# A conditioned residual kernel: loads cut into 8 KB rows, and one ring of pairs split into two

## The chip, the cores and the metric

The kernel runs on one core of a Trainium2 chip. The metric is the device time of one execution in microseconds; three runs of the kernel before gave 642.07, 642.13 and 642.19 us, so the median is 642.13 us. Beside them one execution was taken with the hardware profiler: its own time was 642.29 us and its trace spans 640.4 us from the first instruction to the last.

## What is computed

128 samples of 128 channels by 2048 steps go through two residual channel maps. Each sample picks its own matrix out of 16 for the first and out of 32 for the second; the second adds a bias. Everything is float32.

```python
def _L0_cond_ref(x, weights, condition):
    W = weights[condition]
    return jnp.einsum('bct,bcd->bdt', x, W)

def _L1_cond_ref(x, subjects, weights, biases):
    w = weights[subjects]
    b = biases[subjects]
    out = jnp.einsum('bct,bcd->bdt', x, w)
    return out + jnp.transpose(b, (0, 2, 1))

x = x + _L0_cond_ref(x, L0_cond_weights, itok_B_0_15)            # x: (128, 128, 2048)
x = x + _L1_cond_ref(x, itok_B_0_31, L1_cond_weights, L1_cond_biases)
```

Both maps together are one product per sample with the matrix (I + W0)(I + W1), plus a bias. x is 134.2 MB and is read once; the result is as large and is written once.

## The kernel before

**Pairs and their layout.** The 128 samples are taken two at a time: 64 pairs q, each 2 MB in and 2 MB out. `x_pairs` (line 35) lays a pair over the 128 partitions so that partitions 0 to 63 hold the even sample and 64 to 127 the odd one, and each partition holds two neighbouring channels, which lie side by side in memory: a row of 16 KB. `out_pairs` (line 36) is the same for the stores. A pair lives in one of eight slots of the tile `xt`, 2 x 2048 float32 (16 KB) in each partition. The result of a pair is written into the slot its input came from.

**SyncE (SP, lines 103 to 110)** issues the loads: the two weight tensors, then x pair by pair. The first eight go out at once; each later one waits until the store of the pair eight before it has landed (`stored[slot]`, line 109), since it goes into the same slot.

**GpSimd (POOL, lines 112 to 138)** adds the identity to the two matrices that each sample picks, into `map0T` and `map1`, two pairs deep.

**TensorE (PE, lines 140 to 211)**: `combine` (line 150) multiplies the two matrices of both samples of the next pair into the last 512 columns of `acc1`; ScalarE copies the useful blocks into `both`. `term` (line 158) is one product over 64 channels, 512 steps wide: for each sample k, each half u of the channels and each chunk j of 512 steps, so 16 a pair, two of which (k=0 and k=1) use different halves of the array at the same time. The even sample collects in PSUM tile `acc0`, the odd one in `acc1`. `pair` (line 163) is the order of one pair: eight terms of the low 1024 columns, the combine for the next pair, eight terms of the high columns. A float32 matmul of the program stands as two MATMUL records in the trace, so a pair has 32 records of line 159 and 4 of line 154.

**VectorE (DVE, lines 222 to 233)** moves `acc0` out into `xt` with the bias, two instructions for each half of the columns. **ScalarE (ACT, lines 243 to 267)** does the same with `acc1` (line 251), copies the combined maps (lines 246 and 247), and issues the store of the pair (line 265) when both engines are done with it. At the end it waits for all stores.

The order of the work is written out by hand on every engine; between engines it is set by semaphores. The DMA queue of SP, which carries all x loads, is q1 in the trace, and ACT's, which carries the stores, is q10. Both run on the same 16 DMA engines.

Of the kernel before, what the change touches and what calls it, by code (L numbers as in the profile page):

```python
# [5 lines left out]
def conditioned_residual_kernel(  # L6
# [18 lines left out]
    HC = C // 2  # L25
    CHUNK = 512
    HALF = T // 2
    SLOTS = 8
    PAIRS = B // 2
    TURNS = PAIRS // SLOTS  # L30
# [4 lines left out]
    x_pairs = x.rearrange("(q k) (i u) t -> q (k i) (u t)", k=2, u=2)  # L35
# [3 lines left out]
    with ctx:  # L39
# [20 lines left out]
        map0T = sb("map0T", [C, 2, 2, 2, HC])  # L60
# [22 lines left out]
        maps_ready = [sem(f"maps_ready{s}") for s in range(SLOTS)]  # L83
        combined = sem("combined")
        both_ready = [sem(f"both_ready{s}") for s in range(SLOTS)]
        lo_done0 = sem("lo_done0")
        lo_done1 = sem("lo_done1")
        hi_done0 = sem("hi_done0")
        hi_done1 = sem("hi_done1")

        lo_out = [sem(f"lo_out{s}") for s in range(SLOTS)]
        hi_out = [sem(f"hi_out{s}") for s in range(SLOTS)]
        x_loaded = [sem(f"x_loaded{q}") for q in range(SLOTS)]
        stored = [sem(f"stored{q}") for q in range(SLOTS)]

        w0T_v = w0T_sb[:, :, :].rearrange("p s (i u) -> p s u i", u=2)
# [5 lines left out]
        @block.sync  # L102
        def _(sp):
            sp.dma_start(w0T_sb[:, :, :], w0T).then_inc(w0_loaded, LOAD)
            sp.dma_start(w1_sb[:, :, :], w1).then_inc(w1_loaded, LOAD)
            for q in range(PAIRS):
                slot = q % SLOTS
                if q >= SLOTS:
                    sp.wait_ge(stored[slot], LOAD * (q // SLOTS))
                sp.dma_start(xt[:, slot, :], x_pairs[q, :, :]).then_inc(x_loaded[slot], LOAD)  # L110

        @block.gpsimd
        def _(pool):
# [9 lines left out]
            GROUP = 16  # L123
            for b in range(B):
                if b % GROUP == 0:
                    _, i0 = nc.values_load_multi_w_load_instructions(  # L126
                        cond_sb[0:1, 0, b:b + GROUP], engines=[POOL], min_val=0, max_val=S0 - 1,
                        skip_runtime_bounds_check_because="conditions index the maps")
                    _, i1 = nc.values_load_multi_w_load_instructions(  # L129
                        cond_sb[0:1, 1, b:b + GROUP], engines=[POOL], min_val=0, max_val=S1 - 1,  # L130
                        skip_runtime_bounds_check_because="conditions index the maps")
                q, k = b // 2, b % 2
                if q >= 2 and k == 0:

                    pool.wait_ge(combined, q - 1)
                nc.gpsimd.tensor_tensor(map0T[:, q % 2, :, k, :], w0T_v[:, bass.ds(i0[b % GROUP], 1), :, :], ident_v, ALU.add)  # L136
                nc.gpsimd.tensor_tensor(map1[:, q % 2, k, :, :], w1_v[:, bass.ds(i1[b % GROUP], 1), :, :], ident_v,  # L137
                                        ALU.add).then_inc(maps_ready[q % SLOTS], 1)

        @block.tensor  # L140
        def _(pe):
# [8 lines left out]
            def combine(slot, ready):  # L150

                pe.wait_ge(maps_ready[slot], ready)
                for u in range(2):
                    last = nc.tensor.matmul(acc1[:, CB + u * 2 * C:CB + (u + 1) * 2 * C],  # L154
                                            map0T[:, slot % 2, u, :, :], map1[:, slot % 2, :, :, :], start=True, stop=True)
                last.then_inc(combined, 1)

            def term(acc, k, u, buf, slot, j):
                return nc.tensor.matmul(acc[:, j * CHUNK:(j + 1) * CHUNK], both[k * HC:(k + 1) * HC, buf, u, :],  # L159
                                        xt[k * HC:(k + 1) * HC, slot, u * T + j * CHUNK:u * T + (j + 1) * CHUNK],  # L160
                                        start=u == 0, stop=u == 1)

            def pair(slot, outs, outs_before, next_maps, next_both, loads, begins, ends):

                buf = slot % 2
                prev, next = (slot - 1) % SLOTS, (slot + 1) % SLOTS
                if begins:
                    pe.wait_ge(both_ready[0], 1)

                pe.wait_ge(x_loaded[slot], loads)  # L170
                term(acc0, 0, 0, buf, slot, 0)
                term(acc1, 1, 0, buf, slot, 0)
                term(acc0, 0, 1, buf, slot, 0)
                term(acc1, 1, 1, buf, slot, 0)
                term(acc0, 0, 0, buf, slot, 1)
                term(acc1, 1, 0, buf, slot, 1)
                term(acc0, 0, 1, buf, slot, 1).then_inc(lo_done0, 1)
                term(acc1, 1, 1, buf, slot, 1).then_inc(lo_done1, 1)
                if not begins:
                    pe.wait_ge(hi_out[prev], outs_before)  # L180
                if not ends:
                    combine(next, next_maps)
                term(acc0, 0, 0, buf, slot, 2)
                term(acc1, 1, 0, buf, slot, 2)
                term(acc0, 0, 1, buf, slot, 2)
                term(acc1, 1, 1, buf, slot, 2)
                term(acc0, 0, 0, buf, slot, 3)
                if not ends:

                    pe.wait_ge(both_ready[next], next_both)  # L190
                term(acc1, 1, 0, buf, slot, 3)
                term(acc0, 0, 1, buf, slot, 3).then_inc(hi_done0, 1)
                if not ends:
                    pe.wait_ge(lo_out[slot], outs)
                term(acc1, 1, 1, buf, slot, 3).then_inc(hi_done1, 1)
# [99 lines left out]
```

## Time and profile before

| | |
|---|---|
| median of three runs | 642.13 us |
| profiled execution, its own time | 642.29 us |
| its span | 640.4 us |
| bytes moved by DMA | 271.82 MB, mean 424 GB/s |
| busy share: PE, DVE, ACT, POOL | 84%, 51%, 52%, 19% |
| mean granted TensorE clock | 0.986 of full speed |
| issue to landing, median: x load, store | 24.5 us, 42.9 us |

The page counts an engine as busy while one of its instructions runs. For the DMA engines it gives a share as well: the time of their packets over the time of 16 engines. A packet of this kernel is one row of one partition, and small packets beside them carry the semaphore updates. The clock is full as long as TensorE works; the mean is below one because it falls to half in the last 15 us, when TensorE has nothing left to do.

### The profile page before, as it was taken

What the parts mean: (1) busy time and instruction counts of PE and PEld (TensorE: products, weight loads), DVE (VectorE), ACT (ScalarE), POOL (GpSimd) and SP (SyncE); (2) the same over time, 40 slices, a digit from 0 to 9 for tenths busy, and PEclk for the clock granted to TensorE, in tenths of its full rate; (3) what the DMA queues carried; (4) which work ended last, traced back from release to release, by engine and by line L of the source; (5) the groups of instructions that cost most, each with busy time, mean ns of one, the idle gap of its engine ahead of it and who ended that gap; (6) DMA issues with size and microseconds to landing.
All of it is one profiled execution on the core that took longest, in us unless ns stands there. A gap on an engine that the chain in (4) does not pass through costs nothing.

```text
span 640.4 us, 6061 instructions
## 1 busy us (share of the span) xinstructions
PE 538.4 (84%) x2308; PEld 234.3 (37%) x2308; DVE 329.2 (51%) x259; ACT 333.5 (52%) x385; POOL 124.2 (19%) x263
## 2 busy tenths in 40 slices
PE   1899999999889889888898898888988988988860
PEld 0344444444334333333333333333333333433320
DVE  0266666666554455455545554555455445545550
ACT  0366666666555465455554654555555545545550
POOL 2322222222122122121221221211212212112000
PEclk9999999999999999999999999999999999999995
DMA  8999999999999999999999999999999999999996
GB/s 363 433 415 427 431 432 426 431 433 428 432 433 427 432 434 427 431 434 427 432 434 426 433 435 426 432 433 428 433 431 428 433 431 430 431 433 428 434 429 262
DMA packets 18931, 271.82 MB, mean 424 GB/s; under 512 B 2241, under 2 KB 2274, under 8 KB 2274
## 3 DMA queue, kind: packets, MB, share of 16 engines
q1 hardware_dynamic: 9504, 137.37, 50.3%
q10 hardware_dynamic: 9410, 134.26, 49.0%
q8 instruction: 7, 0.11, 0.1%
q14 instruction: 10, 0.08, 0.0%
HBM read 137.40 MB, written 134.22 MB: 424 GB/s over the span
## 4 chain that ended last, share of the span: by engine, by line
DMA 64%; PE 29%; DVE 3%; POOLq 0%; ACT 0%; issue 0%; DVEq 0%; POOL 0%; SPq 0%; ACTq 0%
DMA out_dram<-xt 40%; PE acc L159 25%; DMA xt<-in_x_dram 23%; PE acc L154 4%; DMA w_sb<-in_w_dram 1%; DVE xt L224 1%; DVE xt L226 1%; DVEq L39 0%; ACT L246 0%; POOLq L126 0%; POOLq L129 0%; POOL map0T L136 0%; POOL map L137 0%; ACT both L247 0%; ACT both L246 0%
## 5 line engine op out<-in xcount | busy, mean ns | idle before, releaser
L159 PE MATMUL acc<-xt,both 64*128 64x512 f32 x2048 | 472.5, 603 | 67.9 <-DMA xt<-in_x_dram 65.7
L251 ACT ACTIVATE xt<-acc,bias_of 64x1024 f32<-64x1024 f32 x256 | 283.7, 1108 | 270.1 <-PE acc L159 267.7
L159 PEld LDWEIGHTS acc<-xt,both 64*128 64x128 f32 x2048 | 189.8, 188 | 319.0 <-issue 211.5
L224 DVE TENSOR_SCALAR xt<-acc,bias_of 64x1024 f32<-64x1024 f32 x128 | 163.3, 1276 | 278.2 <-PE acc L159 278.2
L226 DVE TENSOR_SCALAR xt<-acc,bias_of 64x1024 f32<-64x1024 f32 x128 | 165.0, 1289 | 1.9
L136 POOL TENSOR_TENSOR map0T<-w0T_sb,ident 128x128 f32<-128x128 f32 x128 | 65.6, 513 | 465.8 <-PE acc L154 454.0
L154 PE MATMUL acc<-map,map0T 128*128 128x256 f32 x256 | 73.3, 409 | 1.2 <-POOL map L137 1.2
L137 POOL TENSOR_TENSOR map<-w_sb,ident 128x128 f32<-128x128 f32 x128 | 65.7, 513 | 0.0
L154 PEld LDWEIGHTS acc<-map,map0T 128*128 128x128 f32 x256 | 43.9, 191 | 53.0 <-issue 36.7
L247 ACT ACTIVATE both<-acc 64x256 f32<-64x256 f32 x64 | 24.3, 380 | 0.8
L246 ACT ACTIVATE both<-acc 64x256 f32<-64x256 f32 x64 | 24.2, 377 | 0.8
L246 ACT ACT_TABLE_LOAD x1 | 1.3, 1283 | 17.4 <-PE acc L154 17.4
L145 PE MATMUL acc<-ident,bias_sb 128*32 128x128 f32 x2 | 0.6, 418 | 10.8 <-DMA bias_sb<-in_bias_dram 10.8
L215 DVE TENSOR_TENSOR onehot<-cond_rep,row 32x128 f32<-32x128 int32 x1 | 0.3, 279 | 12.6 <-DMA cond_rep<-in_conds_dram 12.6
L145 PEld LDWEIGHTS acc<-ident,bias_sb 128*32 128x32 f32 x2 | 0.2, 142 | 10.8 <-DMA bias_sb<-in_bias_dram 10.8
L148 PE MATMUL acc<-onehot,biasT 32*128 32x128 f32 x2 | 0.8, 481 | 1.9 <-DVE biasT L217 1.9
L148 PEld LDWEIGHTS acc<-onehot,biasT 32*128 32x128 f32 x2 | 0.5, 304 | 2.3 <-DVE onehot L215 2.3
L219 DVE COPY bias_of<-acc 128x128 f32<-128x128 f32 x1 | 0.3, 292 | 0.9 <-PE acc L148 0.9
L217 DVE COPY biasT<-acc 32x128 f32<-32x128 f32 x1 | 0.3, 278 | 0.0
L117 POOL TENSOR_SCALAR_AFFINE_SELECT ident<-ident 128x128 f32<-128x128 f32 x1 | 0.3, 283 | 0.0
L114 POOL MEMSET ident<- 128x128 f32 x1 | 0.2, 204 | 0.3 <-POOLq L284 0.3
L115 POOL IOTA row<- 32x128 int32 x1 | 0.2, 224 | 0.0
(4 smaller groups left out, 0.4 us busy)
## 6 DMA issues: line engine op xcount, KB each, us to landing
xt<-in_x_dram SPq DMA_DIRECT2D x64, 2048.0 KB, 24.5
out_dram<-xt ACTq DMA_DIRECT2D x64, 2048.0 KB, 42.9
w_sb<-in_w_dram SPq DMA_DIRECT2D x1, 2048.0 KB, 9.4
w0T_sb<-in_w0T_dram SPq DMA_DIRECT2D x1, 1024.0 KB, 4.8
cond_sb<-in_conds_dram ACTq DMA_DIRECT2D x1, 1.0 KB
bias_sb<-in_bias_dram ACTq DMA_DIRECT2D x1, 16.0 KB, 9.4
cond_rep<-in_conds_dram ACTq DMA_DIRECT2D x1, 16.0 KB, 10.8
```

Of the source, the lines that this page charges most:

```text
L117: nc.gpsimd.affine_select(out=ident[:, :], in_=ident[:, :], compare_op=ALU.not_equal, fill=1.0, base=0, pattern=[[-1, C]], channel_multipl ...
L136: nc.gpsimd.tensor_tensor(map0T[:, q % 2, :, k, :], w0T_v[:, bass.ds(i0[b % GROUP], 1), :, :], ident_v, ALU.add)
L137: nc.gpsimd.tensor_tensor(map1[:, q % 2, k, :, :], w1_v[:, bass.ds(i1[b % GROUP], 1), :, :], ident_v, ALU.add).then_inc(maps_ready[q % SLO ...
L145: nc.tensor.matmul(acc0[0:S1, 0:C], bias_sb[:, :], ident[:, :], start=True, stop=True).then_inc(turned, 1)
L148: nc.tensor.matmul(acc1[:, 0:B], biasT[:, :, :], onehot[:, :], start=True, stop=True).then_inc(picked, 1)
L154: last = nc.tensor.matmul(acc1[:, CB + u * 2 * C:CB + (u + 1) * 2 * C], map0T[:, slot % 2, u, :, :], map1[:, slot % 2, :, :, :], start=Tru ...
L159: return nc.tensor.matmul(acc[:, j * CHUNK:(j + 1) * CHUNK], both[k * HC:(k + 1) * HC, buf, u, :], xt[k * HC:(k + 1) * HC, slot, u * T + j ...
L224: nc.vector.tensor_scalar(xt[0:HC, q % SLOTS, a:a + HALF], acc0[0:HC, a:a + HALF], bias_of[0:HC, 2 * q:2 * q + 1], None, ALU.add)
L226: return nc.vector.tensor_scalar(xt[0:HC, q % SLOTS, T + a:T + a + HALF], acc0[HC:C, a:a + HALF], bias_of[HC:C, 2 * q:2 * q + 1], None, AL ...
L246: nc.scalar.activation(both[0:HC, q % 2, :, :], crossed[0:HC, :, 0, :], ACT.Identity)
L247: nc.scalar.activation(both[HC:C, q % 2, :, :], crossed[HC:C, :, 1, :], ACT.Identity).then_inc(both_ready[q % SLOTS], 1)
L251: return nc.scalar.activation(xt[HC:C, q % SLOTS, v * T + a:v * T + a + HALF], acc1[v * HC:(v + 1) * HC, a:a + HALF], ACT.Identity, bias=b ...
```

## The change

The loads and the stores no longer share a buffer. x goes into a tile `xin` of six pairs, in which a partition is one channel and holds both samples of the pair, 2048 steps each: a row in memory is 8 KB, and a pair has 256 of them. Results go into a tile `xout` of four pairs, in the layout of before, with 128 rows of 16 KB. A product now runs over all 128 channels at once: four a sample, eight a pair, one after the other. The combine makes the two 128 x 128 blocks that are used and no others, and ScalarE copies them with one instruction.

SP issues load q when TensorE has finished pair q - 6 (`hi_done1`). TensorE waits before its second product of pair q for the store of pair q - 4. Semaphores for slots become semaphores for twelve places of a group; the loop body on TensorE covers twelve pairs in place of eight, and four pairs follow it.

```diff
-    SLOTS = 8
+    IN, OUT = 6, 4
+    GROUP = 12
...
-    x_pairs = x.rearrange("(q k) (i u) t -> q (k i) (u t)", k=2, u=2)
+    x_pairs = x.rearrange("(q k) c t -> c q k t", k=2)
     out_pairs = out.rearrange("(q k) (i u) t -> q (k i) (u t)", k=2, u=2)
...
-        xt = sb("xt", [C, SLOTS, 2 * T])
+        xin = sb("xin", [C, IN, 2, T])
+        xout = sb("xout", [C, OUT, 2 * T])
...
             for q in range(PAIRS):
-                slot = q % SLOTS
-                if q >= SLOTS:
-                    sp.wait_ge(stored[slot], LOAD * (q // SLOTS))
-                sp.dma_start(xt[:, slot, :], x_pairs[q, :, :]).then_inc(x_loaded[slot], LOAD)
+                if q >= IN:
+
+                    sp.wait_ge(hi_done1, q - IN + 1)
+                sp.dma_start(xin[:, q % IN, :, :], x_pairs[:, q, :, :]).then_inc(x_loaded[q % GROUP], LOAD)
...
-                nc.gpsimd.tensor_tensor(map0T[:, q % 2, :, k, :], w0T_v[:, bass.ds(i0[b % GROUP], 1), :, :], ident_v, ALU.add)
-                nc.gpsimd.tensor_tensor(map1[:, q % 2, k, :, :], w1_v[:, bass.ds(i1[b % GROUP], 1), :, :], ident_v,
-                                        ALU.add).then_inc(maps_ready[q % SLOTS], 1)
+                nc.gpsimd.tensor_tensor(map0T[:, q % 2, k, :], w0T_sb[:, bass.ds(i0[b % BATCH], 1), :], ident[:, :], ALU.add)
+                added = nc.gpsimd.tensor_tensor(map1[:, q % 2, k, :, :], w1_v[:, bass.ds(i1[b % BATCH], 1), :, :], ident_v, ALU.add)
+                if k == 1:
+                    added.then_inc(maps_ready[q % GROUP], 1)
...
+            def combine(k, p):
+                return nc.tensor.matmul(acc1[:, CB + k * C:CB + (k + 1) * C], map0T[:, p % 2, k, :], map1[:, p % 2, k, :, :],
+                                        start=True, stop=True)
+
+            def term(acc, k, p, j):
+                return nc.tensor.matmul(acc[:, j * CHUNK:(j + 1) * CHUNK], both[:, p % 2, k, :],
+                                        xin[:, p % IN, k, j * CHUNK:(j + 1) * CHUNK], start=True, stop=True)
+
+            def pair(p, turn, turn_before, turn_after, loads, stores, begins, ends):
+
+                prev, next = (p - 1) % GROUP, (p + 1) % GROUP
+                if begins and p == 0:
                     pe.wait_ge(both_ready[0], 1)
...
+                pe.wait_ge(x_loaded[p], loads)
+                term(acc0, 0, p, 0)
+                if not (begins and p < OUT):
+
+                    pe.wait_ge(stored[(p - OUT) % GROUP], stores)
+                term(acc0, 0, p, 1).then_inc(lo_done0, 1)
+                if not (begins and p == 0):
+                    pe.wait_ge(hi_out0[prev], turn_before)
+                term(acc0, 0, p, 2)
+                if not ends:
+                    pe.wait_ge(maps_ready[next], turn_after)
+                term(acc0, 0, p, 3).then_inc(hi_done0, 1)
+                if not (begins and p == 0):
+                    pe.wait_ge(hi_out1[prev], turn_before)
+                if not ends:
+                    combine(0, p + 1)
+                    combine(1, p + 1).then_inc(combined, 1)
+                if not (begins and p == 0):
+                    pe.wait_ge(lo_out1[prev], turn_before)
+                term(acc1, 1, p, 0)
+                term(acc1, 1, p, 1).then_inc(lo_done1, 1)
+                if not ends:
+                    pe.wait_ge(lo_out0[p], turn)
+                term(acc1, 1, p, 2)
+                if not ends:
+
+                    pe.wait_ge(both_ready[next], turn_after)
+                term(acc1, 1, p, 3).then_inc(hi_done1, 1)
...
-                nc.scalar.activation(both[0:HC, q % 2, :, :], crossed[0:HC, :, 0, :], ACT.Identity)
-                nc.scalar.activation(both[HC:C, q % 2, :, :], crossed[HC:C, :, 1, :], ACT.Identity).then_inc(both_ready[q % SLOTS], 1)
+                nc.scalar.activation(both[:, q % 2, :, :], acc1[:, CB:CB + 2 * C], ACT.Identity).then_inc(both_ready[q % GROUP], 1)
...
             for q in range(PAIRS):
+                if q < PAIRS - 1:
+                    copy_maps(q + 1)
                 act.wait_ge(lo_done1, q + 1)
                 odd_out(q, 0, 0)
-                if q < PAIRS - 1:
-                    copy_maps(q + 1)
...
                 odd_out(q, 0, HALF)
-                odd_out(q, 1, HALF).then_inc(hi_out[q % SLOTS], 1)
-                act.wait_ge(hi_out[q % SLOTS], 2 * (q // SLOTS + 1))
-                act.dma_start(out_pairs[q, :, :], xt[:, q % SLOTS, :]).then_inc(stored[q % SLOTS], LOAD)
+
+                act.wait_ge(hi_out0[q % GROUP], q // GROUP + 1)
+                odd_out(q, 1, HALF).then_inc(hi_out1[q % GROUP], 1)
+                act.wait_ge(hi_out1[q % GROUP], q // GROUP + 1)
+                act.dma_start(out_pairs[q, :, :], xout[:, q % OUT, :]).then_inc(stored[q % GROUP], LOAD)
```

How the order of instructions changes is shown at two places. The first is TensorE within one pair of the first group (the names behind "waits" are the semaphores, one for each slot or place). Before:

```order
104 L159 MATMUL acc<-xt,both 128x512 [waits x_loaded4]
105 L159 MATMUL acc<-xt,both 128x512 x7
106 L154 MATMUL acc<-map,map0T 128x256 [waits maps_ready5,hi_out3]
107 L154 MATMUL acc<-map,map0T 128x256
108 L159 MATMUL acc<-xt,both 128x512 x5
109 L159 MATMUL acc<-xt,both 128x512 [waits both_ready5]
110 L159 MATMUL acc<-xt,both 128x512
111 L159 MATMUL acc<-xt,both 128x512 [waits lo_out4]
```

Now, for the pair at place 10:

```order
102 L160 MATMUL acc<-xin,both 128x512 [waits x_loaded10]
103 L160 MATMUL acc<-xin,both 128x512 [waits stored6]
104 L160 MATMUL acc<-xin,both 128x512 [waits hi_out0_9]
105 L160 MATMUL acc<-xin,both 128x512 [waits maps_ready11]
106 L156 MATMUL acc<-map,map0T 128x128 [waits hi_out1_9]
107 L156 MATMUL acc<-map,map0T 128x128
108 L160 MATMUL acc<-xin,both 128x512 [waits lo_out1_9]
109 L160 MATMUL acc<-xin,both 128x512
110 L160 MATMUL acc<-xin,both 128x512 [waits lo_out0_10]
111 L160 MATMUL acc<-xin,both 128x512 [waits both_ready11]
```

Sixteen products became eight, the two samples no longer alternate, and the store of four pairs before stands as a wait behind the first product.

The second place is SP's queue of loads. Before:

```order
3 L110 DMA xt<-in_x_dram 128x4096 x8
4 L110 DMA xt<-in_x_dram 128x4096 [waits stored0]
5 L110 DMA xt<-in_x_dram 128x4096 [waits stored1]
6 L110 DMA xt<-in_x_dram 128x4096 [waits stored2]
7 L110 DMA xt<-in_x_dram 128x4096 [waits stored3]
```

Now:

```order
2 L109 DMA w_sb<-in_w_dram 128x4096
3 L114 DMA xin<-in_x_dram 128x2x2048 x6
4 L114 DMA xin<-in_x_dram 128x2x2048 [waits hi_done1] x58
5 L41 UNCONDITIONAL_BRANCH
```

Six loads go out without a wait in place of eight, each is 128 x 2 rows of 2048 elements, and the rest wait for TensorE's last product of a pair and no longer for a store.

## Rows read from the trace of the kernel before

**Rows 1.** The page: packets and bytes; an instruction queue (packets, MB, share of 16 engines).

```profile
DMA packets 18931, 271.82 MB, mean 424 GB/s; under 512 B 2241, under 2 KB 2274, under 8 KB 2274
...
q8 instruction: 7, 0.11, 0.1%
```

**Rows 2.** Busy time by stretch: PE, PEld, DVE, ACT, POOL, clock, DMA share, GB/s.

```profile
200.00:400.00 200.00, 170.98 (x734) 73.53 (x736) 104.25 (x82) 105.15 (x122) 38.53 (x80) 1.00 1.01 431
```

**Rows 3.** Waits: engine, line, releaser; total us, times, longest.

```profile
PE acc L159 <- DMA xt<-in_x_dram: 65.7, 47, 1.5
...
SPq L110 <- DMA out_dram<-xt: 563.2, 56, 42.8
```

**Rows 4.** Timeline, two pairs in mid-run: first products after a load lands.

```profile
308.61 3.70 PE L159 MATMUL acc<-xt,both 64*128 64x512 f32 x16 [1.44 <-DMA xt<-in_x_dram]
...
318.43 3.70 PE L159 MATMUL acc<-xt,both 64*128 64x512 f32 x16 [1.42 <-DMA xt<-in_x_dram]
```

**Rows 5.** Issues: KB each, median us from issue to landing.

```profile
xt<-in_x_dram SPq DMA_DIRECT2D x64, 2048.0 KB, 24.5
out_dram<-xt ACTq DMA_DIRECT2D x64, 2048.0 KB, 42.9
...
w0T_sb<-in_w0T_dram SPq DMA_DIRECT2D x1, 1024.0 KB, 4.8
```

**Rows 6.** Packets, MB, share of 16 engines: 3.2 to 4.7 us (w0T, 8 KB).

```profile
q1 hardware_dynamic: 79, 0.65, 102.7%
```

**Rows 7.** The same from 30 to 32 us (x, 16 KB).

```profile
q1 hardware_dynamic: 55, 0.90, 105.0%
```

**Rows 8.** The same from 100 to 600 us.

```profile
DMA packets 14800, 215.45 MB, mean 431 GB/s; under 512 B 1647, under 2 KB 1647, under 8 KB 1647
...
q10 hardware_dynamic: 7395, 107.79, 50.4%
q1 hardware_dynamic: 7395, 107.55, 50.3%
```

**Rows 9.** Queues in two neighbouring windows of 0.609 us, from 302.436 us.

```profile
q1 hardware_dynamic: 12, 0.20, 75.4%
q10 hardware_dynamic: 4, 0.07, 25.1%
...
q10 hardware_dynamic: 12, 0.18, 69.1%
q1 hardware_dynamic: 5, 0.08, 31.4%
```

**Rows 10.** Chain of waits, its last pieces: start, us, what.

```profile
588.50 24.52 DMA xt<-in_x_dram
...
613.06 7.14 PE acc L159 x31
```

**Rows 11.** Timeline, ScalarE's last store issue.

```profile
622.84 0.34 ACTq L265 DMA_DIRECT2D out_dram<-xt  x1
```

**Rows 12.** One queue from 618 to 623 us; from 636.4 to 637.6 us.

```profile
q10 hardware_dynamic: 149, 2.18, 101.9%
...
q10 hardware_dynamic: 2, 0.03, 6.4%
```

**Rows 13.** Chain of waits at the start: pair 1 on TensorE.

```profile
26.24 1.06 PE acc L154 x4
27.30 7.07 PE acc L159 x32
```

**Rows 14.** Groups by line: busy, mean ns.

```profile
L159 PE MATMUL acc<-xt,both 64*128 64x512 f32 x2048 | 472.5, 603 | 67.9 <-DMA xt<-in_x_dram 65.7
L251 ACT ACTIVATE xt<-acc,bias_of 64x1024 f32<-64x1024 f32 x256 | 283.7, 1108 | 270.1 <-PE acc L159 267.7
```

**Rows 15.** Queue q1 from 36.0 to 36.5 us, when the first store starts.

```profile
q1 hardware_dynamic: 16, 0.26, 196.3%
```

**Rows 16.** Both queues from 6 to 10.3 us, the small transfers of q10 among them.

```profile
DMA packets 256, 1.85 MB, mean 430 GB/s; under 512 B 144, under 2 KB 144, under 8 KB 144
```

More of the change, by code:

```diff
@@ L82, in conditioned_residual_kernel @@
         bias_ready = sem("bias_ready")
-        maps_ready = [sem(f"maps_ready{s}") for s in range(SLOTS)]
         combined = sem("combined")
-        both_ready = [sem(f"both_ready{s}") for s in range(SLOTS)]
         lo_done0 = sem("lo_done0")
+        hi_done0 = sem("hi_done0")
         lo_done1 = sem("lo_done1")
-        hi_done0 = sem("hi_done0")
         hi_done1 = sem("hi_done1")
[L91 to L96, printed above, removed]
+        x_loaded = [sem(f"x_loaded{p}") for p in range(GROUP)]
+        stored = [sem(f"stored{p}") for p in range(GROUP)]
+        maps_ready = [sem(f"maps_ready{p}") for p in range(GROUP)]
+        both_ready = [sem(f"both_ready{p}") for p in range(GROUP)]
+        lo_out0 = [sem(f"lo_out0_{p}") for p in range(GROUP)]
+        hi_out0 = [sem(f"hi_out0_{p}") for p in range(GROUP)]
+        lo_out1 = [sem(f"lo_out1_{p}") for p in range(GROUP)]
+        hi_out1 = [sem(f"hi_out1_{p}") for p in range(GROUP)]
         w1_v = w1_sb[:, :, :].rearrange("p s (i u) -> p s u i", u=2)
@@ L148, in _ @@
             nc.tensor.matmul(acc1[:, 0:B], biasT[:, :, :], onehot[:, :], start=True, stop=True).then_inc(picked, 1)
[L150 to L167, printed above, removed]
-                    pe.wait_ge(both_ready[0], 1)
[L170 to L180, printed above, removed]
-                if not ends:
[L182 to L187, printed above, removed]
-                if not ends:
-                    pe.wait_ge(both_ready[next], next_both)
-                term(acc1, 1, 0, buf, slot, 3)
-                term(acc0, 0, 1, buf, slot, 3).then_inc(hi_done0, 1)
-                if not ends:
-                    pe.wait_ge(lo_out[slot], outs)
-                term(acc1, 1, 1, buf, slot, 3).then_inc(hi_done1, 1)
@@ L197, in group @@
-            def group(twos, twos_before, twos_after, after, now, loads, begins, ends):
-                for s in range(SLOTS):
-                    wraps = s == SLOTS - 1
-                    pair(s, twos, twos_before if s == 0 else twos, twos_after if wraps else twos,
-                         after if wraps else now, loads, begins and s == 0, ends and wraps)
-            pe.wait_ge(bias_ready, 1)
-            combine(0, 2)
-            group(2, 0, 4, 2, 1, LOAD, True, False)
-            with pe.Fori(2, TURNS) as now:
-                group(now * 2, now * 2 - 2, now * 2 + 2, now + 1, now, now * LOAD, False, False)
@@ new lines, in group @@
+            def group(places, now, before, after, loads, loads_before, begins, ends):
+                for p in range(places):
+                    pair(p, now, before if p == 0 else now, after if p == GROUP - 1 else now, loads,
+                         loads_before if p < OUT else loads, begins, ends and p == places - 1)
+            pe.wait_ge(bias_ready, 1)
+            pe.wait_ge(maps_ready[0], 1)
+            combine(0, 0)
+            combine(1, 0).then_inc(combined, 1)
+            group(GROUP, 1, 0, 2, LOAD, 0, True, False)
@@ L211, in _ @@
+            with pe.Fori(2, FULL) as now:
+                group(GROUP, now, now - 1, now + 1, now * LOAD, now * LOAD - LOAD, False, False)
+            group(GROUP, FULL, FULL - 1, FULL + 1, FULL * LOAD, (FULL - 1) * LOAD, False, False)
+            group(REST, FULL + 1, FULL, FULL + 2, (FULL + 1) * LOAD, FULL * LOAD, False, True)
         @block.vector
@@ L230, in _ @@
                 dve.wait_ge(lo_done0, q + 1)
-                even_out(q, 0).then_inc(lo_out[q % SLOTS], 1)
+                even_out(q, 0).then_inc(lo_out0[q % GROUP], 1)
                 dve.wait_ge(hi_done0, q + 1)
-                even_out(q, HALF).then_inc(hi_out[q % SLOTS], 1)
+                even_out(q, HALF).then_inc(hi_out0[q % GROUP], 1)
         @block.scalar
```

27 lines of the change are left out of this document (13 added, 14 removed).

## The prediction

> **What bounds the kernel now.** I read the bytes first. The kernel moves 271.82 MB, a mean of 424 GB/s over the whole span [rows 1]. In mid-run the table by stretch gives a DMA share of 1.01 and 431 GB/s, while TensorE works 171 of 200 us and VectorE and ScalarE about half [rows 2]. So the 16 DMA engines are the bound. The waits agree: TensorE waits for loads and for little else, 47 recorded waits with 65.7 us in all, and SP holds each load back until a store has landed, 563.2 us [rows 3]. From one pair's first product to the next lie 318.43 - 308.61 = 9.82 us [rows 4], and 2 x 2.097 MB at 431 GB/s are 9.73 us: a pair costs what its bytes cost. A slot's life adds up too: 24.5 us for the load, 42.9 for the store [rows 5], about 10 on TensorE and behind it, 77 of the 8 x 9.8 = 79 us that the ring allows. The reader should see that the two queues are never empty.
>
> How the run ends matters next. The last load lands at 613.0 (588.50 + 24.52), TensorE starts at 613.06 [rows 10], and the last store is issued at 622.84 [rows 11]. In these 10 us the DMA engines still run at share 1.02 on stores that are queued [rows 12], but around 637 the share is 6.4%, one engine of 16 [rows 12]. That engine is behind the others, probably through the instruction packets of queues such as q8 [rows 1]. It has work all the time from about 2 us to the end, so every microsecond added to its work, or to its idle time, is added to the span.
>
> **The change part by part.**
>
> *TensorE.* 32 records of 64 rows, two at a time, take 7.07 us a pair, and the four of the combine 1.06 [rows 13]. Now 16 records of 128 rows follow one another. Half as many records, not in twos: 7.07 us if they stream as the old ones do. The combine's records of 128 rows by 256 columns took 1.06 / 4 = 0.265 us [rows 13], against 7.07 / 16 / 2 = 0.221 for the same columns in the big ones, so changing full weights may show some 0.05 us a record: 7.07 + 16 x 0.05 = 7.9. The new combine has half the columns, 0.5 to 0.8 us. A pair is 8.0 to 8.7 us, under 9.82. I take 8.4. The far end, if nothing overlapped, is 16 x 0.603 [rows 14] + 1.1 = 10.8; it is a rival below. The new waits inside a pair are each met earlier: ScalarE needs 4 x 1.108 us [rows 14] a pair and finishes pair q - 1 about 2.7 us into pair q, before the combine is due at 3.5. Cost: nothing, hidden by the DMA.
>
> *The store ring of four.* A store is issued about 10.6 us after its pair began, and TensorE needs it back 4 x 9.82 + 0.4 = 39.7 us after the same point. So a store has 29 us, where it takes 42.9 now [rows 5]. What decides is how the engines share their time between the queues. In two neighbouring windows of one packet time each, q1 has 12 of 16 engines and q10 four, and in the next it is the other way round [rows 9]: an engine changes queue at every row. Rows of 8 KB against rows of 16 KB then give the stores two bytes for each byte of the loads. A store of 8 rows an engine takes 8 x (0.61 + 0.31) = 7.4 us while loads are queued, some 10 to 12 us from issue to landing: well within 29. The ring of four costs nothing.
>
> *The load ring of six.* Load q is issued when TensorE leaves pair q - 6, so it has 6 x 9.82 - 8.4 = 50 us; TensorE will find about five loads outstanding, and never an empty load queue. At the start six loads and the weights (15.7 MB) keep the engines busy from 2 to about 38.5 us; load 6 is issued near 28 and the first store near 31 (pair 0 starts at 19.5, as TensorE's first piece ended at 26.24 [rows 13]). No gap. Cost: nothing.
>
> *Rows of 8 KB.* This is the first real term. The 8 KB packets of w0T take 1.5 us x 16 x 1.027 / 79 = 0.312 us [rows 6]; 16 KB packets take 2 x 16 x 1.050 / 55 = 0.611 [rows 7]. Two small ones cost 0.013 us more than a large one. Each engine has 64 x 8 = 512 large load rows that become 1024 small ones: 512 x 0.013 = 6.7 us at most. The low end is 0: the shares of the steady stretch sum to 100.7% [rows 8], so records overlap a little, and these few packets can't exclude that the overlap hides it. Taking 0.7% of 0.611 = 0.004 off for the one packet more, I get 0.009 x 512 = **4.4 us**, nearer the measured end since the rows measure it.
>
> The Trainium skill (DMA: Bandwidth & Descriptors, section Bandwidth) puts about 10.5 ns on a packet in small transfers; worked out from that page, the term would be an estimate of 5.4 us. The two rows here agree in size.
>
> *The end of the run.* This is the second term. Since stores are now served first, hardly any are queued when the last load lands, at L. Counting from L: store 61 was issued at L - 8.7 and has about 1 us left on the engines. Store 62 is issued at L - 9.8 + 10.9 = L + 1.1. Pair 63 has no combine and takes 7.1 us on TensorE; two ScalarE instructions of 1.108 us follow those of the low half, so its store goes out at L + 9.9, as it did before (622.84 - 613.06 = 9.8). A lone store then takes the 4.8 us of the lone 1 MB load [rows 5] and 2.4 us for the second MB, 7.2: the end is L + 17.1, where it is L + 27.4 now. Of these 17.1 us the engines are busy with 1 + 4.9 + 4.9 = 10.8. So **6 us** (6.3, less some receipt time that both kernels have) are idle that are full today. If two stores were still queued at L it would be 0; if TensorE's pair is slower, up to 8.
>
> *The rest* (POOL's views, one copy of maps in place of two, the longer loop body) is hidden: POOL, VectorE and ScalarE are idle half of the time or more [rows 2].
>
> **Sum.** 640.4 + 4.4 + 6.0 = 650.8 us of span. The median of the runs, 642.13, lies 1.7 us above the span: 652.5 us.
>
> **The rivals.**
>
> A, *stores stay queued*. If an engine shared its time by bytes, TensorE, faster than the DMA at first, would turn queued loads into queued stores up to the ring's limit, and the last stores would cover the end as they do now. Then only the packet term stays: 640.4 + 4.4 + 1.7 = 646.5. The flip of rows 9 speaks against it. The Trainium skill (the same page, section Queues, rings and completion order) states that an engine drains a whole packet of some 9 to 17 descriptors from one ring before it switches, which here would be a whole share of a load or a store and so equal bytes; rows 9 disagree, and the measurement decides. Chance 0.15.
>
> B, *a queue that starts again costs time*. The store queue now empties in each pair. It did so never before; it started once, at 36.0 us, and there 16 packets took 196.3% of half a microsecond of 16 engines, 0.98 us each [rows 15], 0.37 more than 0.611. If each store paid that: 64 x 0.37 = 23.7, 676 us. Against it: q10's small transfers began at 6 to 10 us without a dip, 430 GB/s [rows 16]. It leaves my range above some 0.15 us a pair. Chance 0.10.
>
> C, *TensorE becomes the bound*: 10.8 us a pair from 19.5 on gives some 720 us. It decides above 9.82 us a pair. The combine's own rows overlap their weights, so 0.03.
>
> D, *faster*. Stores alone ran at 436 GB/s [rows 12] against 431 mixed. If the change of direction costs that 1%, and loads that run alone for a quarter of the time, with a queue always five deep, get it back everywhere, the bytes take 623.4 in place of 630.7 us, 7.3 less. It decides where this is more than the idle end; with half of that end covered and no packet cost: 640.4 - 7.3 + 3 + 1.7 = 638. Chance 0.07.
>
> E, *no change*: A without any packet cost, 642.1. Chance 0.07. That the change doesn't make its small rows is no rival: the two samples of a channel lie 1 MB apart.
>
> **How the numbers follow.** My forecast has 0.58. The range runs from E, 642, to both terms at their ends with a tenth of a microsecond of B: 640.4 + 6.7 + 8 + 64 x 0.09 + 1.7 = 662. B in full, C and D, 0.20 in all, are outside. About 0.2% is what a measurement of this kernel can tell from no change; faster is D, 0.07, within it is E, 0.07, slower is the rest, 0.86.
>
> **What the profile after would show.** q1 with some 8,200 more packets and a higher share than q10; the store's landing near 11 us and the load's near 50 (with A, stores stay near 29); a steady rate near 428 GB/s; a gap in the DMA share just after the last load lands, and another before the last store. TensorE's period stays at 9.8 to 9.9 us, with its wait on loads. The prediction is wrong if the two queues still take equal bytes, if the rate falls well under 425 GB/s, or if TensorE no longer waits for loads.

## The result and the profile after

The changed kernel took 649.87 us, the median of six runs from 645.99 to 650.79; the kernel before took 642.12 us beside it (six runs, 642.0 to 642.52). The ratio is 1.0111 with a 95% interval from 1.0095 to 1.0126: slower by 7.75 us, near the 652.5 us that was forecast and inside the range of 642 to 662. The profiled execution took 649.56 us with a span of 647.8 us, 7.4 more than before. The spread is wider as well: 0.5 us between these six runs before, 4.8 us now. That comparison flatters the kernel before, whose runs beside the later experiments lie between 641.96 and 645.56 us.

The page of the changed kernel, with the lines that answer to [rows 1], [rows 5] and [rows 14] (queues: packets, MB, share of 16 engines; issues: KB each, median us to landing; groups: busy us, mean ns, idle before):

```profile
GB/s 359 427 404 427 431 429 433 423 430 432 424 433 426 431 429 425 434 429 425 434 432 430 422 431 426 435 428 424 433 425 434 424 430 424 428 432 425 432 432 150
q1 hardware_dynamic: 17696, 137.37, 50.4%
q10 hardware_dynamic: 9410, 134.26, 48.5%
L160 PE MATMUL acc<-xin,both 128*128 128x512 f32 x1024 | 498.7, 638 | 105.3 <-DMA xin<-in_x_dram 103.5
xin<-in_x_dram SPq DMA_DIRECT2D x64, 2048.0 KB, 47.7
out_dram<-xout ACTq DMA_DIRECT2D x64, 2048.0 KB, 12.0
```

The loads' queue has 8192 packets more than before and the same bytes. A store lands after 12.0 us in place of 42.9, a load after 47.7 in place of 24.5: the stores are served first. One microsecond of mid-run, with both queues at work, shows it directly (304 to 305 us; q10 is the stores, q1 the loads):

```profile
q10 hardware_dynamic: 18, 0.29, 68.8%
q1 hardware_dynamic: 16, 0.13, 30.9%
```

Nearly equal numbers of rows are two bytes of stores for each byte of loads. The mid-run rate is nearly the old one, as the table by stretch shows against [rows 2] (columns as there). Its later rows show the end (us; then PE, PEld, DVE, ACT, POOL, clock, DMA share, GB/s):

```profile
200.00:400.00 200.00, 163.82 (x412) 74.66 (x411) 105.12 (x82) 96.61 (x101) 36.33 (x81) 0.92 1.01 429
...
625.00:630.00 5.00, 1.05 (x2) 0.53 (x3) 0.00 (x0) 0.32 (x1) 0.00 (x0) 0.62 1.00 426
630.00:632.00 2.00, 2.00 (x4) 0.97 (x3) 0.00 (x0) 0.00 (x0) 0.00 (x0) 0.50 0.94 401
632.00:634.00 2.00, 2.00 (x4) 0.73 (x4) 1.23 (x1) 0.00 (x0) 0.00 (x0) 0.75 0.25 107
634.00:636.00 2.00, 2.00 (x6) 0.95 (x5) 1.95 (x3) 0.00 (x0) 0.00 (x0) 1.00 0.00 0
636.00:638.00 2.00, 2.00 (x5) 0.57 (x3) 1.95 (x2) 1.58 (x2) 0.00 (x0) 1.00 0.00 0
638.00:640.00 2.00, 0.09 (x1) 0.00 (x0) 0.00 (x0) 1.96 (x3) 0.00 (x0) 1.00 0.00 0
640.00:648.00 8.00, 0.00 (x0) 0.00 (x0) 0.00 (x0) 0.89 (x1) 0.00 (x0) 0.70 0.61 262
```

Before, the DMA engines were full between the last load's landing and the last store's issue ([rows 12]). Now, from 633.6 to 641.4, nearly 8 us, all sixteen stand still while one pair is computed. The chain of waits names the pieces (start, us, what):

```profile
619.08 3.44 PE acc L160 x8
622.52 6.39 another core or an unknown queue
628.91 0.04 issue
628.95 7.43 PE acc L160 x12
636.38 0.02 issue
636.41 1.11 ACT xout L252
```

The line "unknown queue" is TensorE's wait for load 63, which lands at 628.91, as the first line below says. The last pair's first six products (12 records) then take 7.43 us, and the last store is issued at 640.92:

```profile
628.95 9.13 PE L160 MATMUL acc<-xin,both 128*128 128x512 f32 x16 [6.43 <-DMA xin<-in_x_dram]
636.41 4.48 ACT L252 ACTIVATE xout<-acc,bias_of 64x1024 f32<-64x1024 f32 x4 [11.08 <-PE acc L160]
640.92 0.34 ACTq L268 DMA_DIRECT2D out_dram<-xout  x1
```

The last load lands 18.9 us before the end of the span, where it was 27.4 us [rows 10]. The DMA share from that landing to the end is 0.44 now and was 0.78:

```profile
628.91:647.80 18.89, 9.13 (x16) 3.75 (x16) 5.13 (x4) 4.43 (x4) 0.00 (x0) 0.77 0.44 189
613.02:640.40 27.38, 7.14 (x32) 3.01 (x32) 6.38 (x5) 5.37 (x5) 0.00 (x0) 0.68 0.78 333
```

So on the mean an engine is idle for 0.56 x 18.89 = 10.6 us there, where it was idle for 0.22 x 27.38 = 6.0.

### The profile page after: what moved, and what is told of

Read it like the earlier page. It is cut to its first block, busy times and chain, and to the rows that moved or that the text cites. A ratio compares the mean times of both kernels' runs of the same rounds, so it can differ in the third digit from the quotient of the medians.

```text
span 647.8 us, 3878 instructions
## 1 busy us (share of the span) xinstructions
PE 519.0 (80%) x1284; PEld 236.4 (36%) x1284; DVE 329.2 (51%) x259; ACT 309.6 (48%) x321; POOL 116.7 (18%) x263
## 4 chain that ended last, share of the span: by engine, by line
DMA 52%; PE 37%; another core or an unknown queue 7%; ACT 1%; POOLq 0%; issue 0%; POOL 0%; SPq 0%; ACTq 0%
DMA xin<-in_x_dram 51%; PE acc L160 35%; PE acc L156 2%; DMA w_sb<-in_w_dram 1%; ACT xout L252 1%; ACT L248 0%; POOLq L130 0%; POOLq L133 0%; POOL map0T L140 0%; POOL map L141 0%; ACT both L248 0%; SPq L108 0%; POOLq L140 0%; POOLq L141 0%
## 5 line engine op out<-in xcount | busy, mean ns | idle before, releaser
L160 PE MATMUL acc<-xin,both 128*128 128x512 f32 x1024 | 498.7, 638 | 105.3 <-DMA xin<-in_x_dram 103.5
L160 PEld LDWEIGHTS acc<-xin,both 128*128 128x128 f32 x1024 | 201.9, 206 | 355.2 <-issue 219.3
L252 ACT ACTIVATE xout<-acc,bias_of 64x1024 f32<-64x1024 f32 x256 | 283.7, 1108 | 98.5 <-PE acc L160 95.2
L227 DVE TENSOR_SCALAR xout<-acc,bias_of 64x1024 f32<-64x1024 f32 x128 | 163.3, 1276 | 294.1 <-PE acc L160 292.2
L229 DVE TENSOR_SCALAR xout<-acc,bias_of 64x1024 f32<-64x1024 f32 x128 | 165.1, 1290 | 1.9
L140 POOL TENSOR_TENSOR map0T<-w0T_sb,ident 128x128 f32<-128x128 f32 x128 | 58.2, 455 | 489.1 <-PE acc L156 462.3
L248 ACT ACTIVATE both<-acc 128x256 f32<-128x256 f32 x64 | 24.6, 384 | 216.3 <-PE acc L156 216.3
L156 PEld LDWEIGHTS acc<-map,map0T 128*128 128x128 f32 x256 | 38.9, 193 | 33.4 <-issue 25.3
L156 PE MATMUL acc<-map,map0T 128*128 128x128 f32 x256 | 39.5, 277 | 1.9 <-POOL map L141 1.9
## 6 DMA issues: line engine op xcount, KB each, us to landing
xin<-in_x_dram SPq DMA_DIRECT2D x64, 2048.0 KB, 47.7
```

The source lines that it names most:

```text
L140: nc.gpsimd.tensor_tensor(map0T[:, q % 2, k, :], w0T_sb[:, bass.ds(i0[b % BATCH], 1), :], ident[:, :], ALU.add)
L156: return nc.tensor.matmul(acc1[:, CB + k * C:CB + (k + 1) * C], map0T[:, p % 2, k, :], map1[:, p % 2, k, :, :], start=True, stop=True)
L227: nc.vector.tensor_scalar(xout[0:HC, q % OUT, a:a + HALF], acc0[0:HC, a:a + HALF], bias_of[0:HC, 2 * q:2 * q + 1], None, ALU.add)
L229: return nc.vector.tensor_scalar(xout[0:HC, q % OUT, T + a:T + a + HALF], acc0[HC:C, a:a + HALF], bias_of[HC:C, 2 * q:2 * q + 1], None, AL ...
L248: nc.scalar.activation(both[:, q % 2, :, :], acc1[:, CB:CB + 2 * C], ACT.Identity).then_inc(both_ready[q % GROUP], 1)
L252: return nc.scalar.activation(xout[HC:C, q % OUT, v * T + a:v * T + a + HALF], acc1[v * HC:(v + 1) * HC, a:a + HALF], ACT.Identity, bias=b ...
```

## The experiments

The theory was that an engine changes queue at every row, so that 8 KB loads lose to 16 KB stores, that nothing is then queued when the last load has landed, and that each small row costs a little besides. The rivals were the split rings and the full-height products.

**Small rows alone.** The kernel before, with this edit and the counts of `x_loaded` doubled:

```diff
-                sp.dma_start(xt[:, slot, :], x_pairs[q, :, :]).then_inc(x_loaded[slot], LOAD)
+                sp.dma_start(xt[:, slot, 0:T], x_pairs[q, :, 0:T]).then_inc(x_loaded[slot], LOAD)
+                sp.dma_start(xt[:, slot, T:2 * T], x_pairs[q, :, T:2 * T]).then_inc(x_loaded[slot], LOAD)
```

> The kernel before with one edit: each x load goes out as two DMAs, one for each channel of a partition, so its rows are 8 KB; ring, products and stores are those of before. Theory (rows): the engines change queue at every row, so the 16 KB stores are served first, a store lands 11 to 13 us after its issue (42.9 before), loads land after 55 us or more, nothing is queued when the last load lands, and the DMA engines idle 6 to 8 us before the last store; with some 4 us for 8192 more packets the time is 648 to 651 us. Rival (rings and products): the cost came from the ring of four or from the full-height products, which this kernel does not have: 642 to 645 us, stores landing after about 40 us.

It took 651.54 us (ratio 1.0136, 1.0118 to 1.0154). That is half a microsecond above the expected range. Stores land after 11.6 us, loads after 47.2 (55 or more were expected), and the DMA share falls away at the end. Its page and its table by stretch:

```profile
out_dram<-xt ACTq DMA_DIRECT2D x64, 2048.0 KB, 11.6
...
636.00:638.00 2.00, 2.00 (x10) 0.86 (x8) 0.00 (x0) 0.00 (x0) 0.00 (x0) 0.67 0.39 156
638.00:640.00 2.00, 2.00 (x12) 0.82 (x10) 1.92 (x2) 1.88 (x2) 0.00 (x0) 1.00 0.00 0
640.00:642.00 2.00, 1.47 (x8) 0.38 (x4) 1.14 (x2) 0.80 (x2) 0.00 (x0) 1.00 0.00 0
```

This kernel has one ring of eight and the old products. Small loads alone bring the whole loss and 1.6 us more; the rival is out as the main cause. The surplus is not assigned: the edit also makes 64 DMAs more, with 1024 small packets, which the change does not have.

**Both sides in 8 KB rows.** The tile gets a gap between its two channels, so that neither side can be one row of 16 KB:

```diff
-        xt = sb("xt", [C, SLOTS, 2 * T])
+        TP = T + 16
+        xt = sb("xt", [C, SLOTS, 2, TP])
...
-                sp.dma_start(xt[:, slot, :], x_pairs[q, :, :]).then_inc(x_loaded[slot], LOAD)
+                sp.dma_start(xt[:, slot, :, 0:T], x_pairs[q, :, :, :]).then_inc(x_loaded[slot], LOAD)
...
-                act.dma_start(out_pairs[q, :, :], xt[:, q % SLOTS, :]).then_inc(stored[q % SLOTS], LOAD)
+                act.dma_start(out_pairs[q, :, :, :], xt[:, q % SLOTS, :, 0:T]).then_inc(stored[q % SLOTS], LOAD)
```

> The kernel before with a tile whose two channels lie apart, so that loads and stores both move in 8 KB rows. Theory (rows): with equal rows both queues get equal bytes, landings stay near 24 and 43 us, no gap at the end, and the packet cost is paid twice, 2 x 3.8 us: 649 to 650 us, with a steady rate near 427 GB/s. Rival (only the end costs, a packet costs nothing): 642 to 643 us. Rival (small rows are dear only beside large ones): 642 to 643 us.

It took 646.6 us (1.0062, 1.0045 to 1.0079): 4.4 us above before for 16384 more packets, 2.2 us for the 8192 of the change. Landings are those of before, and no gap opens (issues):

```profile
xt<-in_x_dram SPq DMA_DIRECT2D x64, 2048.0 KB, 25.4
out_dram<-xt ACTq DMA_DIRECT2D x64, 2048.0 KB, 42.7
```

Twice the small rows, and yet 4.9 us faster than with small loads alone, 3.3 us faster than the changed kernel. Neither rival holds: a packet does cost, also beside equals, but less than I expected here (649 to 650 us).

**The changed kernel with 8 KB stores**, `xout` padded in the same way:

> The changed kernel with stores in 8 KB rows as well; rings of six and four and the full-height products stay. Theory (rows): equal bytes for both queues again, so the stores queue up to what the ring of four allows, landing after 24 to 29 us in place of 12, TensorE's pairs come evenly at 9.8 to 9.9 us, and the idle stretch between the last load and the last store goes. The packet cost doubles, so the time is 648 to 651 us, with no gap. Rival (the gap belongs to the rings or to TensorE's order): the gap of 7 us stays and the packets add 4: 653 to 655 us.

It took 645.27 us (1.0037, 1.0023 to 1.0052), 4.6 us less than the changed kernel, although 8192 packets were added. Stores queue up to the ring's limit, 29.6 us (issues), TensorE now waits for stores in place of loads (its last long chain has four pairs in 39.5 us, 9.87 each), and the DMA engines stay mostly busy to the end:

```profile
out_dram<-xout ACTq DMA_DIRECT2D x64, 2048.0 KB, 29.6
...
634.00:636.00 2.00, 0.00 (x0) 0.00 (x0) 0.00 (x0) 1.40 (x2) 0.00 (x0) 0.82 0.80 340
636.00:638.00 2.00, 0.00 (x0) 0.00 (x0) 0.00 (x0) 0.00 (x0) 0.00 (x0) 0.50 0.83 344
```

The theory's mechanism is met, its time was 3 us too high. The rival (the gap belongs to rings or products) is out. The full-height products were not run by themselves; this kernel, which has them, takes 1.3 us less than the kernel before with both sides in 8 KB rows.

**The rings alone**: the kernel before with `xin` of six and `xout` of four pairs, 16 KB rows, the old products:

```diff
-                if q >= SLOTS:
-                    sp.wait_ge(stored[slot], LOAD * (q // SLOTS))
+                if q >= IN:
+                    sp.wait_ge(hi_done0, q - IN + 1)
+                    sp.wait_ge(hi_done1, q - IN + 1)
...
                 pe.wait_ge(x_loaded[slot], loads)
+                if not (begins and slot < OUT):
+                    pe.wait_ge(stored[(slot - OUT) % SLOTS], stores)
```

> The kernel before with the rings of the changed one alone: x into a tile of six pairs, results into a tile of four, loads released by TensorE, stores awaited by TensorE before a pair; rows of 16 KB and the products of before. Theory (rows): equal rows keep some two stores queued to the end: 642 to 643 us, no gap. Rival (the ring of four): the end shows the gap and the time is 646 to 650 us.

It took 644.65 us (1.0036, 1.0013 to 1.006), between the two expectations, and it has a gap of its own (table by stretch):

```profile
625.00:630.00 5.00, 5.00 (x26) 2.30 (x24) 3.94 (x4) 3.55 (x4) 0.00 (x0) 1.00 0.45 190
...
634.00:636.00 2.00, 0.00 (x0) 0.00 (x0) 0.62 (x1) 0.31 (x1) 0.00 (x0) 1.00 0.36 156
```

TensorE holds pair 62 back until a store frees the ring (it starts at 616.75 behind a store that lands at 616.61), and the few stores behind it are gone before pair 63 is done. So a ring of four does cost when stores queue, some 2.4 us here. In the changed kernel they don't queue and it is not waited for.

**The transfers by themselves.** Three kernels that compute nothing: each pair is loaded and stored as it is, in the ring of eight.

> No computation: x is loaded pair by pair into the eight slots and stored again as it is, rows of 16 KB both ways, weights still loaded; the output is x. It measures what the transfers alone take. Theory (rows, DMA-bound): 631 us of bytes at 431 GB/s plus the start of 2 us and some trailing: 636 to 641 us, so the kernel before is at most a few us above its transfers. Rival (an engine holds the kernel before back): well under 636 us.

> The same copy without computation, all rows of x and of the result 8 KB (16384 packets more than the copy with 16 KB rows). Theory (a packet costs a little, 2.2 us for 8192 more, as the kernel before with both in 8 KB rows showed): 4 to 5 us above the copy with 16 KB rows. Rival (the packet times that the records show, 7 to 13 ns each): 8 to 13 us above it.

> The copy without computation with loads in 8 KB rows (two DMAs a pair) and stores in 16 KB rows; the output is x. Theory (a packet costs 2.3 us for 8192, and unequal rows matter only through what is queued at the end): a store follows its load at once, so the end costs a lone store and no more: 636.4 + 2.3 + 2 to 5 = 641 to 644 us. Rival (unequal rows on the two queues cost time in the steady stretch as well, as the lower rate of the mirror image, 426 GB/s, may say): 426 GB/s in mid-run and over 645 us.

| copy | median | against 16 KB rows |
|---|---|---|
| loads and stores 16 KB | 636.42 us | |
| loads 8 KB, stores 16 KB | 639.47 us | +3.05 |
| both 8 KB | 641.02 us | +4.60 |

Both in 8 KB rows cost 4.6 us, 2.3 for 8192 packets, as the second experiment said; the rival that counted the packets' recorded times is out. Unequal rows add only 0.7 us to that (in it are 1024 small packets of 64 more DMAs), less than I expected (641 to 644 us), and the mid-run rate of the mixed copy is the 429 GB/s of the changed kernel:

```profile
DMA packets 22052, 214.74 MB, mean 429 GB/s; under 512 B 2448, under 2 KB 2448, under 8 KB 2448
```

So small loads beside large stores cost little in the steady stretch. They cost where something has to be computed between the last load and the last store: small loads add 9.3 us to the kernel before (651.54 against 642.23) and 3.05 us to the copy.

**The mirror image.** The kernel before with stores in two DMAs of 8 KB rows and loads in 16 KB rows:

> The mirror image: the kernel before with its stores cut into two DMAs of 8 KB rows, loads in 16 KB rows. Theory (an engine changes queue at every row): now the loads are served first, they land after 11 to 14 us and the stores after some 50 to 58, all the last stores are queued when the last load lands, no gap, and only the packet term is paid: 644 to 645.5 us. Rival (mixing two row sizes costs, whichever side is small): 649 to 652 us, as with small loads. Rival (the queue of loads always comes first or last): landings as before.

Loads now land after 12.7 us and stores queue, so which queue comes first does follow the row size, not the queue. There is no gap. But the time was 649.67 us (1.0119, 1.0102 to 1.0136), 4 us above what I expected and inside the range of the first rival, mixing two row sizes costs whichever side is small. Two rows show odd things, the mid-run rate and ScalarE held in issuing a DMA (in the chain of waits):

```profile
DMA packets 21994, 213.16 MB, mean 426 GB/s; under 512 B 2446, under 2 KB 2446, under 8 KB 2446
...
589.79 6.03 ACTq L266
```

The other DMA of the pair takes 0.34 us to issue, this one 6.03 with the store queue long. That delays ScalarE's next work and TensorE behind it, yet the DMA engines stay at share 1.00 meanwhile. About the whole loss is in the rate: 271.8 MB take 638 us at 426 GB/s and 631 at 431. Packets explain some 2 us of that. Where the rest goes (426 against 429) is open, and with it how far that rival holds for small stores: no copy with small stores and large loads was run. For small loads, the side of the change, the mixed copy speaks against it.

**Halving the last store.** If the idle end is paid in full, a shorter last store must show. By sample first: the even half from SyncE when VectorE has it, the odd one from ScalarE.

> The changed kernel with one edit: the result of the last pair is stored in two DMAs, the even sample from SyncE as soon as VectorE has it, the odd one from ScalarE as before. Theory (the idle end is paid in full): the last DMA carries 1 MB in place of 2, so the span ends about 2.4 us earlier: 647 to 648 us. Rival (the end is set by something else, an engine that trails): within 0.5 us of 649.9.

It took 652.19 us (1.0160, 1.0143 to 1.0177), slower by 2.3 us. The table by stretch, and one microsecond of the even half's queue (638 to 639 us), show why:

```profile
632.00:634.00 2.00, 2.00 (x6) 0.92 (x5) 1.97 (x2) 0.11 (x1) 0.00 (x0) 1.00 1.04 442
...
638.00:640.00 2.00, 0.00 (x0) 0.00 (x0) 0.00 (x0) 0.37 (x1) 0.00 (x0) 1.00 1.27 262
...
q1 hardware_dynamic: 16, 0.26, 127.3%
```

In this microsecond 16 packets of 16 KB take 127.3% of 16 engines, 1.273 us each, where one took 0.611 [rows 7]: 16 engines then move 16 x 16.4 KB in 1.273 us, 206 GB/s. The table's 262 is higher because a packet is counted whole in the window in which it starts; by the same reading 442 at share 1.04 is 425. So a DMA of 64 partitions ran at half the rate of one of 128, and a half takes as long as the whole. The odd half, issued at 638.40, lands after 8.8 us, since it also waits behind the even one. The Trainium skill (SBUF — State Buffer, section Door 1: The DMA port swizzle) says that bandwidth depends on how many of the 16 ports the partitions reach, and 64 neighbours reach eight; the trace agrees, 206 against 425 GB/s.

By columns then, all 128 partitions in both:

```diff
+                if q == PAIRS - 1:
+                    act.wait_ge(lo_out0[q % GROUP], q // GROUP + 1)
+                    act.wait_ge(lo_out1[q % GROUP], q // GROUP + 1)
+                    act.dma_start(out_cols[q, :, :, 0:HALF], xout_cols[:, q % OUT, :, 0:HALF]).then_inc(low_stored, LOAD)
```

> The changed kernel; the last pair is stored in two DMAs of all 128 partitions, first the low 1024 columns, when ScalarE has them, then the high ones (rows of 4 KB). Theory (the idle end is paid in full, and the halves by sample failed since a DMA of 64 partitions ran at 262 GB/s): the last DMA has 1 MB at full rate, 2.4 us less: 647 to 648.5 us. Rival (the spread between runs, 646.0 to 650.8, hides it, or the end is set elsewhere): 649 to 651 us.

It took 648.07 us (1.0074, 1.0053 to 1.0095), 1.8 us under the changed kernel where 2.4 were expected; single runs went from 642.67 to 649.55. The gap before it stays, and the last megabyte is short:

```profile
636.00:638.00 2.00, 1.86 (x5) 0.56 (x3) 1.11 (x1) 1.80 (x2) 0.00 (x0) 1.00 0.00 0
638.00:640.00 2.00, 0.00 (x0) 0.00 (x0) 0.00 (x0) 1.23 (x2) 0.00 (x0) 1.00 0.11 47
640.00:642.00 2.00, 0.00 (x0) 0.00 (x0) 0.00 (x0) 1.40 (x2) 0.00 (x0) 0.56 1.03 426
```

It supports that the end is paid nearly in full, but weakly: the two medians come from different sets of runs, and their intervals meet at 1.0095.

**The engine that trails.** The prediction put the last 6 us of the kernel before, in some 5 of which one engine of 16 works alone, down to instruction packets, and the copy has neither the packets nor that stretch. Two kernels tested it, with TensorE's program a third shorter and 2.7 times as long.

> The kernel before with TensorE's last group of eight pairs folded into its loop; for that GpSimd, TensorE and ScalarE make the maps of a 65th pair, which nothing uses. TensorE's program is a third shorter. Theory (the engine that trails at the end is the one that carries the instruction packets; the copy without computation has neither such packets nor a trailing engine and ends 6 us earlier): some 2 of the 7 packets of q8 go, 0.6 us each, so 640.6 to 641.4 us, and the trailing stretch is that much shorter. Rival (the engine trails for another reason): 642.1 to 642.5 us.

> The opposite: the kernel before with TensorE's loop written out, 64 pairs in place of 24 in its program, nothing else changed. Theory (instruction packets on the trailing engine): q8 shows 18 or so packets in place of 7, each 0.6 us on one engine, so 6 to 7 us more: 648 to 649.5 us, all of it in the stretch at the end where one engine works alone. Rival: 642.1 to 643 us.

The shorter program shows 4 packets on q8, the longer one 18 (7 before, [rows 1]):

```profile
q8 instruction: 4, 0.07, 0.0%
...
q8 instruction: 18, 0.29, 0.2%
```

The times are 642.22 us (0.9995, 0.9982 to 1.0009) and 642.24 us (0.9996, 0.9987 to 1.0006) against 642.43 for the kernel before. TensorE's instruction packets are not what the run ends on; my inference falls. In the longer program the DMA share at 634 to 636 is 0.59 in place of 0.19 in the shorter one, so the additional bytes do not all lie on the engine that ends last. Why one engine trails is open. None of these kernels that compute the result beats the kernel before beyond its noise.

## Why the prediction was right, and where it was not

**What bounds, and the direction.** The bytes bound both kernels, and the two terms named, small packets and an idle end, are the ones that the experiments found. Small loads alone give the whole loss; equal rows take 4.6 us of it back in spite of more packets. The forecast of 652.5 us is 2.6 above the measured 649.87 because both terms were put too high.

**Rows 9, an engine changes queue at every row.** Right. The landings were forecast at 11 and 50 us and are 12.0 and 47.7, and rows are served in equal numbers (18 and 16 above); the landings swap sides when the row sizes do. The rule that rival A takes from the Trainium skill (DMA: Bandwidth & Descriptors, section Queues, rings and completion order), a whole packet of descriptors from one ring before a switch, does not describe these queues.

**Rows of 8 KB: the term was mis-sized.** It was put at 4.4 us from recorded packet times and measures 2.2 (kernel) and 2.3 (copy). The step that failed took the difference of 0.013 us between two 8 KB records and one of 16 KB and removed 0.004 for overlap. A record's time is not the spacing between packets; 2.25 us over 512 rows an engine is 0.004 us a row. The 10.5 ns a packet of the Trainium skill (DMA: Bandwidth & Descriptors, section Bandwidth), an estimate of 5.4 us, is further off. The row that would have sized it is a rate over a long stretch of small packets, and the trace of before had only 1 MB of them.

**The end: right in kind, some parts off.** Predicted were 6.0 us. The two rows by share above give 10.6 - 6.0 = 4.6 us. What the span grew by beyond the packets is 7.4 - 2.2 = 5.2 us, and 7.75 - 2.25 = 5.5 by the medians; by this account the 0.6 us between 4.6 and 5.2 lie in the transfers, about what unequal rows add to the copy (0.7).

The parts differ from the forecast. The last store was issued 12.0 us after the last load's landing (640.92 - 628.91), not 9.9: TensorE had waited 6.4 us, its clock is recorded at 0.50 of full speed from 630 to 632, and six products took 7.43 us where 128 x 512 pieces at full clock take 6.87 for eight, so 5.15 for six. These 2.3 us of clock are the difference. The idle stretch of all engines was nearly 8 us, in one piece: store 62 was issued at 625.36, 3.6 us ahead of the landing, where I had put it 1.1 us behind with a gap ahead of it, and stores 61 and 62 filled the time up to 633.6. Against that stands the trailing engine: before, it worked alone for some 5 us, and now none does, since the last store runs on all sixteen (share 1.22 at 646.0 to 646.5, 0.02 behind it). I had counted the whole stretch before as full. So the sentence that every microsecond added to the trailing engine is added to the span is wrong here, and that the term came near 6.0 us is in part luck: a longer idle stretch stands against a tail that vanished.

**TensorE's period: wrong, and it mattered.** I wrote 9.8 to 9.9 us evenly. TensorE has fewer and longer waits for loads, 31 with 103.5 us in all and up to 6.6 each, where it had 47 with 65.7 and up to 1.5 [rows 3]. The chain shows pairs of 7.3 us in a row and then a wait (waits as in [rows 3]; chain: start, us, what):

```profile
PE acc L160 <- DMA xin<-in_x_dram: 103.5, 31, 6.6
...
597.09 6.87 PE acc L160 x16
603.96 0.45 PE acc L156 x4
604.40 6.87 PE acc L160 x16
611.27 0.44 PE acc L156 x4
611.72 6.92 PE acc L160 x16
```

A plausible course is that a landed load makes a store, which holds back the loads behind it, until TensorE has nothing and the loads catch up together. That is argued, not shown. What the traces show is that small loads bring the irregular pairs: with them alone TensorE waits up to 5.2 us for a load, and with both sides of the changed kernel in 8 KB rows the longest wait is 2.3 us. The spread of the runs does not follow this: it is 4.8 us for the changed kernel, 0.8 for the kernel before with both sides in 8 KB rows, but 3.7 for the changed kernel with both (643.59 to 647.26), whose pairs come evenly. Its cause is open. TensorE's own cost was below the 8.4 us taken: 6.87 + 0.45 = 7.3 us a pair. The 0.05 us a record that I had added for changing full weights did not show (6.87 / 16 = 0.43 us a record). As DMA is the bound, this cost the forecast nothing, and rival C is out.

**Rivals.** A's premise was refuted by the landings. Part of its arithmetic is in doubt too: with a ring of four, queued stores did not cover the whole end in the rings-alone kernel (2.4 us lost), though they nearly did in the changed kernel with 8 KB stores. B, a price for each start of the store queue, is out: the mixed copy keeps 429 GB/s with stores that land in 11.2 us. D did not show: no kernel here passed 431 GB/s in mid-run. E is out by the interval of the ratio, 1.0095 to 1.0126.

## What to carry to other kernels

When two DMA queues share the engines, compare their row sizes. Here, with rows of 8 and 16 KB, service went row by row: the queue with the larger rows got two bytes for one and its transfers landed sooner (after 12.0 us, the others after 47.7), and that decided what was still queued when the last input landed. A DMA-bound kernel pays for its last load's computing unless enough stores are waiting at that moment; size the rows, and the output ring, for the end of the run and not only for the middle. And size a packet's price from the rate of a copy, not from the records of packets.

## What the runs showed of the hardware that was not expected

A DMA over 64 partitions took 1.273 us for each 16 KB packet in place of 0.611, so 16 engines moved 206 GB/s where 128 partitions gave 425. Eleven more instruction packets on q8 (18 with 0.29 MB in place of 7) did not change the time (642.24 against 642.43 us). Issuing a DMA held ScalarE for 6.03 us, in place of 0.34, while the store queue was long. After a wait of 6.4 us TensorE's recorded clock was at half, 1.2 of 2.4 GHz, from 630 to 632 us, which put 2.3 us (7.43 against 5.15) into a stretch on which the whole kernel waited.
